# Graph network block: chunks of node features transposed once, unsplit, instead of high and low part each

## The reference, cut to what matters

```python
# x: 625 x 512, 20625 edges (src, dst), 128 features an edge
h = relu(layernorm(x)); x = x + L0(h)    # edge MLP, message sum over edges, node MLP
h = relu(layernorm(x)); x = x + L1(h)
h = relu(layernorm(x)); x = x + L2(h)    # one graph convolution
h = relu(layernorm(x)); x = x + L3(h)    # three graph convolutions, one linear

def L1(feat):                            # the stage that the change touches
    h = relu(feat @ W_init.T)
    for l in range(3):
        fwd = mean_agg(h, src, dst) @ W_fwd[l].T
        bwd = mean_agg(h, dst, src) @ W_bwd[l].T
        h = relu(concatenate((h, fwd, bwd), axis=1) @ W_self[l].T)
    return h
```

## Time and profile before

| | |
|---|---|
| median of the runs shown | 1199.06 us |
| profiled execution, its own time | 1200.69 us |
| its span, first to last instruction | 1198.9 us, mean granted TensorE clock 0.989 |
| busy: TensorE matmul, weight load | 97%, 81% |
| busy: VectorE, ScalarE, POOL | 71%, 57%, 35% |
| chain that ended last, by engine | PE 88%, DVE 6%, ACT 3%, issue 1%, DMA 1% |

### The profile page before, as it was taken

The page is one execution under the profiler, slowest core; times in us unless marked ns, Lnnn a source line. Parts: engine busy times, 40 slices in busy tenths (PEclk is TensorE's granted clock), DMA queues, the critical chain, the costliest instruction groups (busy, mean ns, idle before and its releaser), DMA issues.

```text
span 1198.9 us, 20918 instructions
## 1 busy us (share of the span) xinstructions
PE 1158.1 (97%) x6268; PEld 970.2 (81%) x6268; DVE 851.5 (71%) x1479; ACT 680.5 (57%) x1351; POOL 418.6 (35%) x546
## 2 busy tenths in 40 slices
PE   6989899999999999999999999998899999999997
PEld 3658788888888888888888888886789888798786
DVE  8767777777777777777777777777977234175664
ACT  3567567676676766767676676765734223142352
POOL 2001555565546555555555555551500000001000
PEclk9999999999999999999999999999899999999999
DMA  5544622222222222222222322221101202022101
GB/s 192 205 154 158 234 87 72 83 82 71 87 74 79 80 74 85 70 85 77 76 85 68 87 74 79 82 72 36 44 1 37 71 8 97 0 71 71 44 2 44
DMA packets 26966, 95.88 MB, mean 80 GB/s; under 512 B 6533, under 2 KB 6783, under 8 KB 22578
## 3 DMA queue, kind: packets, MB, share of 16 engines
q0 software_dynamic: 18592, 54.42, 15.2%
q1 hardware_dynamic: 8208, 40.84, 9.5%
q10 hardware_dynamic: 130, 0.13, 0.0%
HBM read 86.52 MB, written 8.85 MB: 80 GB/s over the span
## 4 chain that ended last, share of the span: by engine, by line
PE 88%; DVE 6%; ACT 3%; issue 1%; DMA 1%; DVEq 0%; SPq 0%; ACTq 0%
PE ps L1004 13%; PE ps L1006 12%; PE ps L1005 12%; PE ps L997 9%; PE ps L999 9%; PE ps L998 9%; PE ps L1012 3%; PE ps L1011 3%; PE ps L1111 3%; PE ps L1110 3%; PE ps L1050 3%; PE ps L1115 2%; PE ps L1038 1%; PE ps L1247 1%; PE ps L1065 1%
## 5 line engine op out<-in xcount | busy, mean ns | idle before, releaser
L1004 PE MATMUL ps<-we_hi,s_hi 128*128 128x512 f32 x664 | 268.7, 405 | 0.0
L1006 PE MATMUL ps<-we_hi,s_lo 128*128 128x512 f32 x664 | 260.2, 392 | 0.0
L1005 PE MATMUL ps<-we_lo,s_hi 128*128 128x512 f32 x664 | 260.1, 392 | 0.0
L578 POOL DMA_INDIRECT xg<-h_dram,node_picks x166 | 177.0, 1066 | 96.7 <-POOL node_picks L568 66.1
L720 ACT ACTIVATE m_hi<-msg 128x512 fp32r<-128x512 f32 x166 | 105.0, 632 | 156.9 <-DVE msg L1667 92.9
L572 POOL DMA_INDIRECT rbf<-in_edge,edge_picks x166 | 171.5, 1033 | 50.5 <-issue 33.5
L1672 DVE TENSOR_TENSOR m_lo<-msg,m_hi 128x512 fp32r<-128x512 f32 x166 | 114.9, 692 | 59.3 <-ACT m_hi L720 58.6
L1660 DVE TENSOR_TENSOR s_lo<-s,s_hi 128x1024 fp32r<-128x1024 f32 x83 | 101.8, 1226 | 75.5 <-ACT s_hi L714 50.3
L1006 PEld LDWEIGHTS ps<-we_hi,s_lo 128*128 128x128 f32 x664 | 124.9, 188 | 28.6
L1005 PEld LDWEIGHTS ps<-we_lo,s_hi 128*128 128x128 f32 x664 | 125.7, 189 | 21.1
L1004 PEld LDWEIGHTS ps<-we_hi,s_hi 128*128 128x128 f32 x664 | 125.3, 189 | 21.4
(11 more groups left out here) (301 smaller groups left out, 2556.4 us busy)
## 6 DMA issues: line engine op xcount, KB each, us to landing
stage<-in_fold_a SPq DMA_DIRECT2D x6, 1024.0 KB, 5.1
stage<-in_fold_b SPq DMA_DIRECT2D x6, 1024.0 KB, 8.6
fold_dram<-folded SPq DMA_DIRECT2D x6, 1024.0 KB
wstage<-fold_dram SPq DMA_DIRECT2D x6, 1024.0 KB, 4.9
w_raw<-in_nodew SPq DMA_DIRECT2D x3, 1024.0 KB, 7.2
wstage<-in_selfw SPq DMA_DIRECT2D x3, 1024.0 KB, 5.0
rbf<-in_edge,edge_picks POOLq DMA_INDIRECT x166
xg<-h_dram,node_picks POOLq DMA_INDIRECT x166
```

What stands on the lines that cost most here:

```text
L578: pool.indirect_dma_start(xg[t.slot][:, j], None, h_dram, bass.IndirectOffsetOnAxis(ap=node_picks[t.slot][:, j:j + 1], axis=0)).then_inc(x ...
L1004: pe.matmul(outp, lh, rh, start=False, stop=False, skip_group_check=True)
L1005: pe.matmul(outp, lh, rl, start=False, stop=False, skip_group_check=True)
L1006: return pe.matmul(outp, ll, rh, start=False, stop=False, skip_group_check=True)
```

## The change

Output chunks of `h1` and of layers 0 and 1 are evicted differently: ScalarE writes the rectified chunk unsplit into one of two row buffers (`h_ring`, the memory of `row_a` and `row_b`), waits for itself, and copies it to `h_hi`. TensorE transposes the row buffer once, from the moment it is written. ScalarE copies the result to `ht_hi` and VectorE writes `ht_lo` as PSUM minus `ht_hi`. A turn takes one unit instead of two, so `h1` has 17 units instead of 22 and a layer 26 instead of 31, ScalarE counts one output more for each output chunk, and the bank numbers and waits shift. As the row buffers are used until layer 1 is over, both bias broadcasts are issued directly before load 7 (j = 3 * LAYERS - 2).

```diff
-    return ("back", c, 2)
+    return ("back", c, 1)
...
-        _at += 2
+        _at += 1
...
-LAYER_UNITS, LAYER_ACTS = 31, 26
+LAYER_UNITS, LAYER_ACTS = 26, 31
...
+        h_ring = (row_a, row_b)
...
                 if j == 0:
                     sp.wait_ge(filled, UNIT["aggT"] + 1)
-                    sp.dma_start(row_a[:], a["b2"].to_broadcast([P, F])).then_inc(bias2_in, 16)
                 if j:
                     sp.wait_ge(w_split, 2 * j)
+                if j == 3 * LAYERS - 2:
+                    sp.dma_start(row_a[:], a["b2"].to_broadcast([P, F])).then_inc(bias2_in, 16)
+                    sp.dma_start(row_b[:], a["b4"].to_broadcast([P, F])).then_inc(bias4_in, 16)
...
-            sp.wait_ge(res_ready, 2 * C)
-            sp.dma_start(row_b[:], a["b4"].to_broadcast([P, F])).then_inc(bias4_in, 16)
...
# ScalarE, h1 and (with the layer's counts) out_and_turned
-                    act.activation(h_hi[:, c], bank(u)[0:NC], ACT.Relu).then_inc(act_done, 1)
+                    act.activation(h_ring[c % 2][0:NC], bank(u)[0:NC], ACT.Relu).then_inc(act_done, 1)
+                    act.wait_ge(act_done, H1_AT["lin", c][1] - 1)
+                    act.activation(h_hi[:, c], h_ring[c % 2][0:NC], ACT.Copy).then_inc(act_done, 1)
...
# TensorE
-            def turn_back(c, unit_of, at):
-                for part, src in enumerate((h_hi, h_lo)):
-                    b = unit_of(at + part)
-                    for k in range(K):
-                        mm = pe.transpose(b[:, k * NC:k * NC + NC],
-                                          src[:, c, k * P:k * P + P].bitcast(F32), ident[0:NC, 0:NC])
-                    mm.then_inc(filled, 1)
...
-                    pe.wait_ge(freed, count(OUT_AT[c] + 1))
-                    turn_back(c, unit_of, at)
+                    pe.wait_ge(act_done, acts(woven_acts(WOVEN.index(("out", c, OUT_AT[c]))) + 1))
+                    turn_chunk(unit_of(at), h_ring[c % 2][0:NC])
...
                 def layer_unit(n):
-                    pe.wait_ge(freed, count(n - 6 if n < 8 else n - 7))
+                    pe.wait_ge(freed, count(n - 1 if n < 2 else n - 7))
                     return ps[:, n % 8]
...
# VectorE, h1; the layers likewise
-                    dve.wait_ge(filled, u + 2)
-                    dve.wait_ge(act_done, done)
-                    dve.tensor_copy(ht_lo[:, :, n], bank(u + 1)[:, 0:K * NC].rearrange("p (k n) -> p k n", k=K)).then_inc(freed, 2)
+                    turned_lo((u, done), c)
```

More of the change, by code:

```diff
@@ L59 @@
 UNITS = [("aggT", 5, 5), ("mlp1", 8, 16), ("adjT", 10, 10), ("mlp2", 5, 0), ("large", 4, 0), ("degrow", 2, 0),
-         ("h1", 22, 15), ("layer0", 31, 26), ("layer1", 31, 26), ("layer2", 22, 16), ("mid2", 11, 10), ("conv2", 4, 4),
+         ("h1", 17, 20), ("layer0", 26, 31), ("layer1", 26, 31), ("layer2", 22, 16), ("mid2", 11, 10), ("conv2", 4, 4),
          ("mid3", 11, 11), ("conv_a", 4, 8), ("lin_b", 5, 5), ("conv_b", 2, 4), ("lin_c", 5, 5), ("conv_c", 2, 4),
@@ L109, with woven_acts, places @@
     _u, _a = _u + _units, _a + _acts
-LAYER_UNITS, LAYER_ACTS = 31, 26
-assert UNIT["layer0"] % 8 == 0
-def places(stage, woven_parts, without_act):
+LAYER_UNITS, LAYER_ACTS = 26, 31
+def woven_acts(n):
+    return n + sum(what == "out" for what, _, _ in WOVEN[:n])
+def places(stage, woven_parts, without_act, with_two=None):
     where, acts = {}, ACTS[stage]
     for what, c, at in woven_parts:
-        acts += what != without_act
+        acts += (what != without_act) + (what == with_two)
         where[what, c] = (UNIT[stage] + at, acts)
     return where
-H1_AT, MID2_AT, MID3_AT = places("h1", H1, "degrees"), places("mid2", MID, "product"), places("mid3", MID, None)
-BANK = {u: u % 8 for u in range(UNIT["layer0"])}
+H1_AT, MID2_AT, MID3_AT = places("h1", H1, "degrees", "lin"), places("mid2", MID, "product"), places("mid3", MID, None)
+BANK = {u: (u - UNIT["layer0"]) % 8 for u in range(UNIT["layer0"])}
 BANK.update({u: (u - UNIT["layer2"]) % 8 for u in range(UNIT["layer2"], UNIT["lin_b"])})
@@ L852, in _, with out_and_turned @@
                     act.wait_ge(filled, u + 1)
-                    act.activation(h_hi[:, c], bank(u)[0:NC], ACT.Relu).then_inc(act_done, 1)
+                    act.activation(h_ring[c % 2][0:NC], bank(u)[0:NC], ACT.Relu).then_inc(act_done, 1)
+                    act.wait_ge(act_done, H1_AT["lin", c][1] - 1)
+                    act.activation(h_hi[:, c], h_ring[c % 2][0:NC], ACT.Copy).then_inc(act_done, 1)
                 elif what != "degrees":
                     turned_hi(u, c)
-            def out_and_turned(count, bank_of):
-                for what, c, at in WOVEN:
+            def out_and_turned(count, bank_of, acts):
+                for i, (what, c, at) in enumerate(WOVEN):
                     act.wait_ge(filled, count(at + 1))
@@ L862, in out_and_turned @@
                     if what == "out":
-                        act.activation(h_hi[:, c], b[0:NC], ACT.Relu).then_inc(act_done, 1)
+                        act.activation(h_ring[c % 2][0:NC], b[0:NC], ACT.Relu).then_inc(act_done, 1)
+                        act.wait_ge(act_done, acts(woven_acts(i) + 1))
+                        act.activation(h_hi[:, c], h_ring[c % 2][0:NC], ACT.Copy).then_inc(act_done, 1)
                     else:
@@ L888, in layer @@
                     return
-                out_and_turned(lambda n: count(16 + n), lambda n: ps[:, (16 + n) % 8])
+                out_and_turned(lambda n: count(16 + n), lambda n: ps[:, (16 + n) % 8],
+                               lambda n: l * LAYER_ACTS + (ACTS["layer0"] + 16 + n))
             with act.Fori(0, LAYERS - 1) as l:
@@ L1241, in _, with out_and_turn @@
                 column_sums(unit(UNIT["degrow"] + i), 0, i)
-            def turn_back(c, unit_of, at):
-                for part, src in enumerate((h_hi, h_lo)):
-                    b = unit_of(at + part)
-                    for k in range(K):
-                        mm = pe.transpose(b[:, k * NC:k * NC + NC],
-                                          src[:, c, k * P:k * P + P].bitcast(F32), ident[0:NC, 0:NC])
-                    mm.then_inc(filled, 1)
-            def out_and_turn(count, unit_of, out_chunk):
-                for what, c, at in WOVEN:
+            def out_and_turn(count, unit_of, out_chunk, acts):
+                for i, (what, c, at) in enumerate(WOVEN):
                     if what == "out":
@@ L1278, in _ @@
                 else:
-                    pe.wait_ge(freed, H1_AT["lin", c][0] + 1)
-                    turn_back(c, unit, u)
+                    pe.wait_ge(act_done, H1_AT["lin", c][1] - 1)
+                    turn_chunk(unit(u), h_ring[c % 2][0:NC])
             def layer(l, last, by_adj):
@@ L1322, in layer @@
                     return out_chunk
-                out_and_turn(lambda n: count(16 + n), lambda n: layer_unit(16 + n), out_chunk)
+                out_and_turn(lambda n: count(16 + n), lambda n: layer_unit(16 + n), out_chunk,
+                             lambda n: l * LAYER_ACTS + (ACTS["layer0"] + 16 + n))
             conv_flat = (conv_hi, conv_lo)
@@ L1864, in out_and_turned @@
                     if what == "out":
-                        dve.wait_ge(act_done, acts(i + 1))
+                        dve.wait_ge(act_done, acts(woven_acts(i + 1)))
                         dve.scalar_tensor_tensor(out=h_lo[:, c], in0=bank_of(at)[0:NC], scalar=0.0, in1=h_hi[:, c],
@@ L1868, in out_and_turned @@
                     else:
[L1869 to L1872, removed]
+                        n = slice(c * NC, c * NC + NC)
+                        dve.wait_ge(act_done, acts(woven_acts(i + 1)))
+                        dve.tensor_tensor(ht_lo[:, :, n], bank_of(at)[:, 0:K * NC].rearrange("p (k n) -> p k n", k=K),
+                                          ht_hi[:, :, n], op=ALU.subtract).then_inc(freed, 1)
             def layer(l, last):
```

## The result

The changed kernel took 1202.77 us (median of 9 runs, 1200.87 to 1203.68) against 1199.06 for the kernel before: a ratio of 1.003, 95% interval 1.0019 to 1.004. It is 3.7 us slower; 1200.8 was forecast, with a range of 1197.8 to 1203.3.

A forecast was written before the change was run, and what follows sets the result against it. TensorE was taken as the bound (busy 97% of the span, 88% of the chain). Layers 0 and 1 -1.76, `h1` +1.12 and bias loads +2.33 gave +1.7 us: 1200.8 us for the median, range 1197.8 to 1203.3.

The forecast's parts named there:

- Transposes and middle chunks, ends of layers: Layers 0 and 1: middle turns save 1.29 us, the end starts products 0.41 later; -0.88 a layer, -1.76 for two.
- the held bank of unit 0: Layer ends: turn 3 sits in the bank of the next layer's unit 0, so products wait for its `ht_lo`, 0.41 us later.
- three middle turns: Layers 0 and 1: turns 0, 1 and 2 save 0.43 us each by fewer transposes, 1.29 us a layer.
- h1: Stage `h1`: `h_lo` comes 0.65 us later and passes through nearly full VectorE; first product of layer 0 +1.12 us.
- The round through VectorE: Stage `h1`: `h_lo`, a reciprocal and two `ht_lo`, 3.8 us a round, hold `lin(2)` until 896.02, not 895.57.
- The broadcasts: Layer 2: both bias loads queued on SP ahead of load 7 delay it 3.0 us; TensorE waits +2.33 us.
- D: Layer 2: delay of load 7 by both bias broadcasts, between 2.84 and 4.54 us, taken as 3.0.
- TensorE's wait of +2.33: Layer 2, before the third part of output 0: D less 0.67 us absorbed, +2.33 us (ends 1.3 and 3.9).
- rival 4: Layer 2: the new pause drops the clock from 2.4 to 1.2 GHz, 1.7 us of work; +3.4, 1202.4 us; chance 0.15.
- rivals 3 and 4: Rival 4 has its own line; the other: both broadcasts in layer 2 at full price, total +3.2, 1202.3 us; chance 0.18.

The follow-up runs named there:

- two-units run: The changed kernel with a turn counted as two units again (22 and 31 units, the old spacing of banks); 1196.93 us, ratio 0.999 to the kernel before.
- all repairs: The changed kernel with broadcasts behind load 8, two units a turn, h1's reciprocals behind `ht_lo`, and ScalarE reading PSUM twice; 1190.22 us, ratio 0.9937 to the kernel before.

## Why the prediction was right and where it fell short

- *Transposes and middle chunks, ends of layers:* -0.88 a layer forecast, -0.86 measured in layer 1 (69.15 against 70.01); the product at 3.12 forecast, 3.05 and 3.15 measured; the held bank of unit 0 confirmed by the two-units run. The pitch of the trace held: with the end 0.44 later, three middle turns gave their 1.29. By the figure of the Trainium skill, "TensorE: Matmul & The Clock Gate", Part 4 (about 275 ns a transpose, for another type), they would have given an estimated 3.3 a layer if a transpose occupied TensorE that long. The trace agrees with the figure as a duration (270 ns listed for a single transpose) and not as what one occupies (0.107 us from start to start).
- *h1:* +1.12 forecast, +0.92 measured (+0.8 to +1.1 over the profiles with this stage unchanged). The round through VectorE was right to 0.01 us at `lin(2)`. What I did not see is how much of it was the reciprocals' place alone: with them moved h1 is 19.41, 1.2 us shorter than before.
- *The broadcasts:* D of 3.0 forecast, 3.09 measured in the change (2.54 to 3.09 over the variants); the first 2.28 (2.27 forecast), the second 0.26 to 0.81 (0.57 forecast). TensorE's wait of +2.33 was a little too large: layer 2 without a fall is 30.5 to 31.0 in the seven variants that have both broadcasts and no fall in that stretch, +1.8 to +2.3 over 28.7. By the Trainium skill, "DMA: Bandwidth & Descriptors", the section on the anatomy of one DMA, whose figures are for DMAs that GpSimd issues, D would have been an estimated 2.0 for both (I had written 2.05; two times 0.60 and issues of 0.37 and 0.43 make 2.00). One broadcast alone already took 2.28.
- *What failed:* rival 4's place. I weighed a clock fall only behind the new pause in layer 2 and ruled the layer ends out because the clock had "stayed through the layer ends" of the kernel before. There TensorE's waits were 0.56 to 0.63 us; my own sum made them longer (3.12 from 2.71, with four transposes fewer inside), and put two new waits into h1, and I did not ask the clock's question again of these. The sum had nothing for them; the runs show two falls, at 910 and 1050 us, 1.5 us each: +3.0. Behind the new pause in layer 2, where rival 4 had put its fall, the changed kernel has none.

With them the account closes: +0.95 (h1), -1.72 (layers), +2.0 (broadcasts), +3.0 (falls) = +4.2, against +3.7 and +4.2 by the medians of two comparisons. Without the falls it is +1.2 where I had +1.7. The rest, which the sum left alone, was 0.7 shorter in the changed kernel's profile, so a few tenths of the agreement are chance. The time lies inside the range of 1197.8 to 1203.3, but outside the forecast's own 1199.2 to 1202, and the case given the best chance, within 0.2% of before, was not what came, but slower by 0.3%. In this the range was lucky: its upper part was there for rivals 3 and 4 (1202.3 and 1202.4), neither of which happened as told, and the two falls that filled it were in neither.

## What to carry to other kernels

Removing half of the transposes on the path helps only if the chain that feeds the next product does not grow longer for it: here 0.65 us more on ScalarE went through VectorE's queue, a shared bank and a reciprocal to TensorE, each of them cheap to mend once named. Mended together they turned +3.7 us into -8.1, of which 5.3 lie in the stages that they touch. Where a sum lengthens a wait of TensorE by tenths of a microsecond, ask of every such wait what the clock will do, not only of the largest new one: here waits of 1.3 us were followed by falls and one of 2.1 us was not. And count matmuls in a stretch, since a busy share of 4.00 of 4.00 hides the lower clock. And a load without slack should not get anything queued ahead of it on its issuing engine: one broadcast there cost 2.28 us.

## What the runs showed of the hardware that I had not expected

- A fall at 1050 us came in four profiles, each with a fall at 910 and a pause of 1.35 us before 1050; with the pause but no fall at 910 (two profiles) there was none, and a pause of 1.25 us at 980 never brought one. The falls of one profile begin 139.95 us apart in all four, however the pauses lie. Whether the earlier fall or the place in time decides is open.
- A 256 KB broadcast ahead of a 1 MB load delayed it by 2.28 us, two by 2.54 to 3.09: the first is dear, the second cheap.
- ScalarE starts a second Relu from PSUM 0.50 us after the first (888.61, 889.11, all repairs), and a Copy that depends on the first 0.63 after it (977.28, 977.91, the changed kernel).
